# Seven basis units before the softmax in place of two value tiles, one value tile in each of the first four attention steps, and a new front

## The reference

```
h = relu(layernorm(x));  x = x + layer(h)
L0  q, k, v = h Wq + bq, h Wk + bk, h Wv + bv        8 heads of 64
    attn = softmax(q k^T / 8, masked by the edges);  o = attn v Wo + bo
    h1 = layernorm(h + o);  layernorm(h1 + relu(h1 W1 + b1) W2 + b2)
L1  GIN: prelu(h lin^T); twice: (x + sum over edges) -> two linears, batch norm, relu
L2  GCN: normalised sum over edges, W, leaky relu
L3  two RGCN layers, 2 relations: w[r] = sum_b att[r, b] basis[b]   (30 bases of 512 x 512)
    messages gate(x_j) * x_j w[r], summed over edges, + x root + bias
```

## Time and profile before

| | |
|---|---|
| median of 3 runs | 458.7 us (457.14 to 459.46) |
| the profiled execution | 456.62 us, span 454.8 us |
| instructions | 6200 |
| PE busy | 438.6 us, 96% |
| DVE busy | 346.3 us, 76% |
| ACT busy | 243.7 us, 54% |
| granted clock of TensorE | full in all 40 slices |
| HBM read | 93.5 MB |

### The profile page before, as it was taken

How to read it: one execution, slowest core, us unless ns; L and a number is a source line. 1 busy time by engine, 2 the same in 40 slices (tenths; PEclk the granted TensorE clock), 3 DMA queues, 4 the chain that set the end, 5 groups by cost and what they waited for, 6 DMA issues and landing times.

```text
span 454.8 us, 6200 instructions
## 1 busy us (share of the span) xinstructions
PE 438.6 (96%) x2226; PEld 274.3 (60%) x2226; DVE 346.3 (76%) x736; ACT 243.7 (54%) x428; POOL 42.9 (9%) x59
## 2 busy tenths in 40 slices
PE   8999999899997899999999999999998999999997
PEld 3334554443432346768776866677465788888885
DVE  5999996899999968688779657675759695866212
ACT  5999994676897617543345436544534623511210
POOL 3240000024223011000010000010000000000000
PEclk9999999999999999999999999999999999999999
DMA  7997347426699859978099766777973550000002
GB/s 254 415 398 176 110 174 308 179 93 219 235 380 353 295 206 332 409 272 345 11 372 404 295 246 251 275 252 267 375 199 115 225 186 1 1 0 2 0 3 92
DMA packets 18090, 99.22 MB, mean 218 GB/s; under 512 B 2959, under 2 KB 3599, under 8 KB 7567
## 3 DMA queue, kind: packets, MB, share of 16 engines
q1 hardware_dynamic: 13191, 72.72, 43.4%
q0 software_dynamic: 4000, 25.18, 15.1%
q10 hardware_dynamic: 864, 0.86, 0.6%
HBM read 93.50 MB, written 5.25 MB: 217 GB/s over the span
## 4 chain that ended last, share of the span: by engine, by line
PE 70%; DVE 12%; DMA 8%; issue 8%; ACT 1%; POOL 0%; DVEq 0%; POOLq 0%
PE bank L1371 15%; PE sbank L1703 10%; PE bank L1716 6%; PE sbank L1357 6%; PE sbank L1427 6%; PE bank L1608 5%; DMA bring<-in_basis 4%; PE bank L1688 4%; PE sbank L1567 3%; PE bank L1450 3%; DMA wring<-in_weights 3%; PE bank L1357 3%; PE bank L1513 2%; PE sbank L1337 2%; PE sbank L1490 2%
## 5 line engine op out<-in xcount | busy, mean ns | idle before, releaser
L839 DVE TENSOR_SCALAR cnt<-iota_row,edge_f 128x512 bf16<-128x512 f16 x132 | 41.4, 350 | 0.4 <-PE sbank L1427 0.4
L1357 PE MATMUL sbank<-bring,attw 120*32 120x512 f32 x336 | 41.0, 599 | 0.1
L1427 PE MATMUL sbank<-cnt,adjT 128*128 128x512 bf16 x132 | 30.6, 380 | 0.3
L466 ACT ACTIVATE stat<-stat,eps 128x1 f32<-128x1 f32 x32 | 9.4, 294 | 39.3 <-DVE stat L858 39.3
L576 ACT ACTIVATE adjT<-distance,edge_w,edge_f 128x128 bf16<-128x128 bf16 x61 | 29.2, 479 | 1.4 <-PE sbank L1427 1.4
L1281 DVE SCALAR_TENSOR_TENSOR y_lo<-sbank,gate,y_hi 128x512 fp32r<-128x512 f32 x16 | 11.8, 750 | 22.6 <-ACT y_hi L765 22.5
L497 ACT ACTIVATE s<-bank,colsb 128x512 f32<-128x512 f32 x24 | 16.4, 687 | 21.8 <-PE bank L1371 21.8
L1427 PEld LDWEIGHTS sbank<-cnt,adjT 128*128 128x128 bf16 x132 | 12.3, 98 | 21.7 <-DVE cnt L839 6.4
L529 ACT ACTIVATE distance<-iota_row,edge_f 128x128 bf16<-128x128 f16 x61 | 24.3, 400 | 1.8 <-DVE edge_f L905 0.4
L1371 PE MATMUL bank<-hT_hi,w_hi 128*128 128x512 f32 x64 | 25.3, 395 | 0.0
L1371 PE MATMUL bank<-hT_hi,w_lo 128*128 128x512 f32 x64 | 24.9, 390 | 0.0
(11 more groups left out here) (250 smaller groups left out, 1092.5 us busy)
## 6 DMA issues: line engine op xcount, KB each, us to landing
bring<-in_basis SPq DMA_DIRECT2D x59, 1024.0 KB, 9.8
wring<-in_weights POOLq DMA_DIRECT2D x8, 1024.0 KB, 10.0
landing<-in_weights POOLq DMA_DIRECT2D x4, 1024.0 KB, 5.1
w_scratch<-stage SPq DMA_DIRECT2D x16, 256.0 KB
hT<-in_weights POOLq DMA_DIRECT2D x4, 1024.0 KB, 9.1
qkw<-w_scratch POOLq DMA_DIRECT2D x2, 2048.0 KB, 7.9
rring<-in_rows POOLq DMA_DIRECT2D x12, 256.0 KB, 8.5
wring<-in_basis SPq DMA_DIRECT2D x2, 1024.0 KB, 12.9
```

The costliest lines, as they stand in the source:

```text
L839: dve.tensor_scalar(hot_s[:, n % HOT, :], iota[:, :], src_f[:, n:n + 1], None, ALU.is_equal).then_inc(sem("hot_ready"), 1)
L1357: mm = pe.matmul(unit_bank(b)[32 * j:32 * j + 32, :], attw[0:KB, u // UNITS, g, :], unit_place(u)[0:KB, j, :], start=(g == 0), stop=(g == ...
L1427: pe.matmul(bank[7][:, :], hot_d[:, n % HOT, :], hot_s[:, n % HOT, :], start=(n == 0), stop=(n == ECH - 1)).then_inc(sem("hot_used"), 1)
```

## The change

1. **Front.** All four x tiles go on SP's queue. ACT's queue carries dst, then src (semaphore `edges_loaded`), then the edge type, which now counts on `cols_loaded`. DVE does four of the eight edge steps ahead of the norm statistics, after waiting for dst and src.
2. **Units for value tiles.** `FIRST_UNITS = (4, 3)`: four units stand between `products(0, 0)` and `exclude(0, 0)`, and three after the count check, where value tiles 0 and 1 stood. The value tiles go to steps 0 to 3, one each, all in bank 3; `STEP_UNITS` becomes (2, 0, 0, 0, 3, 3, 3, 0). The sum of units up to the end of the attention is the same (26). Batch 3 has bank 1. The first unit of batch 5 waits for all value tiles.
3. **DVE, ACT and POOL of it.** `take_v(it-1)` stands in steps 1 to 4, after the sum over heads and ahead of `find_max`. ACT copies batches 2 and 3 in step 0, behind the exponentials of step 1. `attend(0)` waits for batch 3's copy. The load of row g2 on POOL moves behind step 4.
4. **GCN.** `units(6)` stands for `units(5)` and `keep_clock(4)`; a later `units(2)` is `units(1)`. The GCN product goes tile by tile (`BY_TILE`). The low part of root1 is made on POOL (`low_parts`), not on DVE.

```diff
-STEP_UNITS = (1, 2, 3, 3, 3, 3, 3, 0)
+FIRST_UNITS = (4, 3)
+STEP_UNITS = (2, 0, 0, 0, 3, 3, 3, 0)
 def unit_bank(b):
+            if b == EARLY_UNITS // BATCH + 1:
+                return bank[1]
 # SP
-                for c in (0, 2):
+                for c in range(C):
                     sp.dma_start(xr[:, c, :], x[:, c, :]).then_inc(sem(f"x{c}_loaded"), 16)
 # POOL
+                def low_parts(name, ks=range(C)):
+                    hi, lo = weight_parts(name)
+                    i = IN_PARTS.index(name)
+                    for k in ks:
+                        pool.wait_ge(sem("weight_hi"), i * C + k + 1)
+                        if i and k == 0:
+                            pool.wait_ge(sem("weight_parts"), i * C)
+                        pool.tensor_tensor(lo[:, k, :], weight(name)[:, k, :], hi[:, k, :].bitcast(F32),
+                                           ALU.subtract).then_inc(sem("weight_parts"), 1)
...
-                scale_heads(0)
-                scale_heads(1)
-                load_row("g2", "v")
-                for it in range(2, 2 * C - 1):
+                for it in range(2 * C - 1):
                     scale_heads(it)
+                    if it == C:
+                        load_row("g2", "v")
...
                 load_weight("root1")
+                low_parts("root1")
                 load_w(0)
 # ACT
-                for c in (1, 3):
-                    act.dma_start(xr[:, c, :], x[:, c, :]).then_inc(sem(f"x{c}_loaded"), 16)
-                for i, e in enumerate((src, dst, etype)):
+                for i, e in ((1, dst), (0, src)):
                     act.dma_start(edge_i[:, i, :], e).then_inc(sem("edges_loaded"), 16)
+                act.dma_start(edge_i[:, 2, :], etype).then_inc(sem("cols_loaded"), 16)
...
-                    stage_units(STEP_UNITS[it])
+                    stage_units(STEP_UNITS[it] + (0 if it else sum(FIRST_UNITS)))
 # DVE, ahead of the norm statistics
+                dve.wait_ge(sem("edges_loaded"), 32)
+                ... (dst & 127, dst >> 7, src_f, then dst_lo; taken out of their place below)
...
                 centre(0)
-                take_v(0)
-                take_v(1)
                 for it in range(2 * C):
...
+                    if 1 <= it <= C:
+                        take_v(it - 1)
...
-                    if it < 2:
-                        take_v(2 + it)
...
                     T_lo("agg2", c)
-                split_weight("root1")
 # PE
-                        if g == 0 and b == EARLY_UNITS // BATCH:
-                            pe.wait_ge(sem("v"), 1)
-                        elif g == 0 and b == EARLY_UNITS // BATCH + 1:
+                        if g == 0 and b == EARLY_UNITS // BATCH + 3:
                             pe.wait_ge(sem("v"), C)
...
                 products(0, 0)
-                qkv_tile(2 * C)
+                units(FIRST_UNITS[0])
                 pe.wait_ge(sem("no_edge"), 1)
                 exclude(0, 0, "scores_psum")
...
-                qkv_tile(2 * C + 1)
+                units(FIRST_UNITS[1])
                 pe.wait_ge(sem("flag"), 1)
...
-                    if it:
+                    if it == 0:
+                        units(1)
+                    else:
+                        if it == 1:
+                            pe.wait_ge(sem("stage_ready"), EARLY_UNITS // BATCH + 2)
                         attend(it - 1)
...
-                    if it < 2:
-                        qkv_tile(2 * C + 2 + it)
-                    units(STEP_UNITS[it])
+                    if it < C:
+                        qkv_tile(2 * C + it)
+                    units(STEP_UNITS[it] - (it == 0))
...
-                units(5)
-                keep_clock(4, bank[4])
+                units(6)
...
-                parts_stage("gcn", hT_parts, "agg2", "gcn_psum", t_major=False)
+                parts_stage("gcn", hT_parts, "agg2", "gcn_psum", order=BY_TILE, t_major=False)
...
-                units(2)
+                units(1)
                 turn_rel(0, "h_rel0", 1)
```

More of the change, by code:

```diff
@@ L90 @@
 RING_UNITS = [n for n in range(2 * UNITS) if not in_extra(n)]
-STEP_UNITS = (1, 2, 3, 3, 3, 3, 3, 0)
-ATTENTION_BATCHES = (EARLY_UNITS + sum(STEP_UNITS)) // BATCH + 1
+FIRST_UNITS = (4, 3)
+STEP_UNITS = (2, 0, 0, 0, 3, 3, 3, 0)
+ATTENTION_BATCHES = (EARLY_UNITS + sum(FIRST_UNITS) + sum(STEP_UNITS)) // BATCH + 1
 AGG0_BATCHES = 11
@@ L293, in wait_unit @@
             pe.wait_ge(sem(f"basis{r % BATCH}_loaded"), 16 * (r // BATCH + 1))
-        def v_bank(c):
-            return 3 if c else 2
         def place_of(h):
@@ L583, in _ @@
                         if t == 0:
-                            act.wait_ge(sem("cols_loaded"), 32)
+                            act.wait_ge(sem("cols_loaded"), 48)
                         qk_take(t)
@@ L874, in take_v @@
                     dve.wait_ge(sem("v_psum"), c + 1)
-                    dve.tensor_tensor(vr[:, c, :], bank[v_bank(c)][:, :], row("bv"), ALU.add).then_inc(sem("v"), 1)
+                    dve.tensor_tensor(vr[:, c, :], bank[3][:, :], row("bv"), ALU.add).then_inc(sem("v"), 1)
+                dve.wait_ge(sem("edges_loaded"), 32)
+                dve.tensor_scalar(dst_part[:, 0, :], edge_i[:, 1, :], P - 1, None, ALU.bitwise_and).then_inc(
+                    sem("edge_step"), 1)
+                dve.tensor_scalar(dst_part[:, 1, :], edge_i[:, 1, :], P.bit_length() - 1, None,
+                                  ALU.logical_shift_right).then_inc(sem("edge_step"), 1)
+                dve.tensor_copy(src_f, edge_i[:, 0, :]).then_inc(sem("edge_step"), 1)
+                dve.wait_ge(sem("edge_step"), 3)
+                dve.tensor_copy(dst_lo, dst_part[:, 0, :]).then_inc(sem("edge_step"), 1)
                 for c in range(C):
@@ L888, in _ @@
                                     bank[c][:, :].rearrange("p (f n) -> p f n", f=C)).then_inc(sem("hT0"), 1)
[L890 to L895, removed]
+                dve.wait_ge(sem("cols_loaded"), 48)
                 dve.tensor_scalar(rel1, edge_i[:, 2, :], 0.0, None, ALU.not_equal).then_inc(sem("edge_step"), 1)
-                dve.wait_ge(sem("edge_step"), 4)
-                dve.tensor_copy(dst_lo, dst_part[:, 0, :]).then_inc(sem("edge_step"), 1)
+                dve.wait_ge(sem("edge_step"), 5)
                 dve.scalar_tensor_tensor(field, rel1, float(C), dst_part[:, 1, :], ALU.mult, ALU.add).then_inc(
@@ L918, in _ @@
                         dve.tensor_scalar(never[:, :], ident[:, :], NEVER, None, ALU.mult).then_inc(sem("never_bq8"), 1)
-                        dve.wait_ge(sem("cols_loaded"), 32)
+                        dve.wait_ge(sem("cols_loaded"), 48)
                         dve.tensor_scalar(bq8[:, :], col("bq", 0, C), HD ** -0.5, None, ALU.mult).then_inc(
@@ L1438, in qkv_tile @@
                     elif which:
-                        pe.wait_ge(*((sem("v"), c) if c >= 2 else (sem("k"), C)))
-                    at = v_bank(c) if which == 2 else c
+                        pe.wait_ge(*((sem("v"), c) if c else (sem("k"), C)))
+                    at = 3 if which == 2 else c
                     if which == 1:
@@ L1476, in _ @@
                 NH = N // 2
-                pe.wait_ge(sem("cols_loaded"), 32)
+                pe.wait_ge(sem("cols_loaded"), 48)
                 def products(it, pair):
```

## The result

The changed kernel takes 470.12 us (median of 4 runs, 468.55 to 470.46), the one before 459.08 in the runs beside it: a ratio of 1.0234, 95% interval 1.0209 to 1.026, some 11 us slower. The forecast was 459.6, its range ended at 462.0.

What follows compares the result with a forecast made beforehand. PE was taken as busy 438.6 of 454.8 us, with DVE setting the attention's pace. Front -0.4, attention +1.5 and GCN -0.2 summed to +0.9 us: 459.6 us for the median, eight in ten between 455.7 and 462.0.

Steps and rivals of the forecast that it cites:

- Front: From start to first one-hot: reordered edge steps and loads give -0.4 us (bounds -0.6 and +0.3), carried over whole.
- GCN: GCN part: unit 60's wait is nearly offset by DVE's earlier first tile; -0.2 us, bounds -2.6 and +1.
- Three waits: PE gaps claimed at unit 11's load, ACT's copy before unit 16, and unit 60's load: 1.9, 2.4, 3.1 us.
- The step that failed: End of attention: DVE's last step opens 4.7 us late, its last product ends 1.5 late; attention sum +1.5 us.
- The lateness itself: DVE's attention steps: the last, step 7, was to open at 153.9 against 149.2, 4.7 us late.
- about 88.1: Before step 1's scores: time unit 14's load was to land, queued behind units 11 to 13.
- rival (b): New PE gaps drop the clock, one or two warm-ups; +2.8 to +4.7 us, 461.5 to 463.4; chance 0.12.
- It decides from the gap at unit 60: GCN part: the 3.1 us PE gap at unit 60 was to decide whether the clock drops.
- A refill alone takes 4.7, and 3.8 us of waits go: Attention steps 4 to 6: ring full by 105, four of nine units already loaded, so old load waits of 3.8 us vanish.
- It costs nothing if they land before x: DVE's head: the new wait for dst and src was allowed 0 to 0.5 us, being small loads first on their queue.
- The gain of -2.6: GCN part without unit 60's wait: product ends at 347.5 instead of 350.1; the lower bound of that term.

Runs made afterwards that it cites:

- e14: Kernel before with the attention edits (item 2, 3), but FIRST_UNITS (3, 3) and STEP_UNITS (2, 1, 1, 1, 3, 2, 2, 0): ratio 1.0152 to the kernel before.
- e18: e14 with ACT's copy take_ao(1) moved ahead of root(1, 1): ratio 1.0045 to the kernel before.
- e16: The changed kernel with ACT's copy take_ao(1) moved ahead of root(1, 1): ratio 1.0204 to the kernel before.
- e10: Kernel before with the attention edits alone, plus matmuls on zeros ahead of units 11, 12, 14, 16 and project(2): ratio 1.0147 to the kernel before.
- e2: Kernel before with the attention edits alone (units for value tiles, with their DVE, ACT and POOL edits): ratio 1.0208.
- e4: The changed kernel with matmuls on zeros in five PE waits (front, units 11, 14, 16, 60): 465.76 us, ratio 1.0165 to the kernel before.
- e1: Kernel before with the front edits alone (queues of x, edges and edge type; four edge steps ahead of the statistics): ratio 1.0033.
- e5: Kernel before with only the front's new DMA queues, DVE's order as it was: ratio 1.0029.
- e11: Kernel before with all GCN edits, plus 14 matmuls on zeros ahead of unit 60: ratio 1.0002.
- e6: Kernel before with only the GCN tile order and POOL's low parts, units and zeros as before: ratio 0.9964.
- e17: Kernel before with ACT's copy take_ao(1) moved ahead of root(1, 1): ratio 0.9986.
- e9: Kernel before with the last unit of step 6 (unit 25) moved behind attend(7): ratio 1.0019.
- e8: Kernel before with the attention edits, but FIRST_UNITS (3, 3) and STEP_UNITS (2, 1, 0, 0, 3, 3, 3, 0): ratio 1.0098.
- e12: Kernel before with only root1's low part on POOL in place of DVE, GCN product in its old order: ratio 0.9988.

## Why the prediction was wrong

**Three waits were read right.** Predicted 1.9 us for unit 11, 2.4 for the copy ahead of unit 16, 3.1 for unit 60; measured 2.02, 2.25, 3.37.

**The step that failed:** "Behind it 3.7, 1.9 and 3.7 us (project, attend, project) lie before `attend(7)`, and DVE's last product ends 6.9 after the opening, at 160.8; it starts there, where it started at 159.3. Sum for the attention: +1.5 us". There 4.7 us of lateness on DVE became 1.5 by slack on PE. The reckoning ended one instruction too soon: behind `attend(7)` comes `project(2)`, which waits for ACT behind DVE's statistics, 13.1 us after the opening in nine kernels. This chain had no slack, and lateness passes on whole. That is the 3.2 us, shown by the table and by e14 and e18. In the changed kernel itself PE had no slack either: late unit loads kept `project(0)` until 160.50, some 2.4 us behind DVE's release (in e14 that comes 2.55 us ahead of the last opening), so PE's own work would have let `project(2)` start only 1.2 us earlier, about what e16 gained. In e14, without those load waits, the chain alone holds PE by 3.1.

**The lateness itself was mis-sized.** From `products(0, 0)` on, the changed kernel's last opening is 11.45 - 2.67 = 8.8 us late (products at 77.70 for 75.03), not 4.7. The openings between, at 95.39, 103.70, 116.02 and so on, tell where. The second is 3.0 late, predicted 1.2: unit 14 is there at 92.88 - 2.67 = 90.2, not at "about 88.1", and step 1's scores stand behind it. That isn't the clock: in e10 this opening is 2.8 late too (100.83 for 98.00). Step 1 takes 12.3 us for the 10.9 predicted, and this is the clock, since e10 has 10.98. Steps 2 to 6 take 44.7 for 43.8. Together 4.7 + 1.8 + 1.4 + 0.9 = 8.8. (e2, whose clock was full in step 1, has 11.05 there.)

**The clock** was rival (b), at a chance of 0.12 and with one or two warm-ups. The profiled execution had four, and gaps of 2.0 to 2.3 us, about what I had computed for the attention (1.9 and 2.4), were enough. One costs less than I had from the earlier trace rows: 3.2 to 4.4 us for all of them (e4), about 1 each and not 1.9. Which gaps cost also changes between executions: that of e16 has the same front and no drop there. The step wrong here is "It decides from the gap at unit 60".

**The late loads.** "A refill alone takes 4.7, and 3.8 us of waits go": no wait stands between 130 and 149, but waits of 1.00 and 1.33 us come at 150.05 and 159.50. The ring is full from 109 on and its loads start only when units are used again. e14 shows the cure, and that it is worth nothing while DVE's chain holds `project(2)`.

**Front.** Predicted -0.4, measured +1.4 (e1). "It costs nothing if they land before x": DVE got src at 6.41 us (5.77 in e1), while x's statistics start at 4.36 in e5, with the same queues. Everything on DVE stood behind that wait, PE waited 2.46 us for the first turn, and the first one-hot came 2.0 us later (14.06 for 12.04), not half a us earlier; in e1 it came 1.4 later. The quarter size of the load said nothing of when it lands. That this wait is all of the +1.4 isn't shown, since e5, without it, measured nearly the same time.

**GCN.** Predicted -0.2, measured +0.6 (0.9995 to 1.0052), and 1.0002 with the clock up (e11): without the drop of the clock the sum was right. The gain of -2.6 that was expected without unit 60's wait was 1.6 (e6). POOL took 5.95 us for its four parts (predicted 4.8), and DVE's add took 1.66 beside it in place of 0.69. By the Trainium skill's GPSIMD Engine Reference (section 1) they share the interface for two SBUF inputs; the run agrees, by 1.0 us on one instruction. It doesn't undo the gain (e6).

**The sum again**, by what the runs gave: front +1.4; attention +6.8 by DVE's last opening without the clock (e10: 156.08 for 149.23), passed on whole, and +2.8 by the clock; GCN +0.6. That is 11.6 for the measured 11. The two profiled executions differ by more, 13.6 us. Some 0.9 of it lies between 225 and 250, where PE takes 17.4 us in place of 16.5 from a group of four units to the last turn of the stage (236.46 to 253.86, before 225.04 to 241.58). That isn't the change: e17, which moves one line of ACT, takes 17.7, and 17 of the 20 traces take 17.2 or more. The profiled execution of the kernel before, 2.1 us under its median, is one of the three quick ones.

## What to carry to other kernels

Before crediting slack on one engine, follow each late event to the end of every chain that starts in it, also past the instruction that was late before: two chains that end within 0.2 us of each other look like one in a profile, and moving either alone gained nothing here. Price a new gap on TensorE at its length plus a possible clock drop, even at 2 us, and keep idle filler where a real unit of work would have to wait for its load. A wait placed at the head of an engine's order delays all that stands behind it until its load lands, however small the load is. Before reading a difference of 1 us between two profiles, look for it in a third kernel that doesn't have the change.

## What the runs showed of the hardware

- In the changed kernel gaps of 2.02, 2.25, 2.46 and 3.37 us were followed by the lower clock, one of 2.23 wasn't. In e9 one of 2.10 was, in e8 one of 2.59, in e14 one of 2.67; but in e1 one of 2.67 and in e16 one of 2.87, both behind the zeros of the front, were not (the next eight matmuls took 1.27 us, in the changed kernel 1.94). In the profiled execution of e12 the clock fell after waits of 1.47, 0.92 and 1.31 us for loads, with units between them (`project(0)` took 5.94 us for 3.70). Length alone doesn't decide.
- A load of 66 KB (src) issued at 1.19 us was there 5.2 us later in the changed kernel and 4.6 in e1; a tile of x four times as large, issued at 0.74 on the other queue, was there after 3.6 (e5, DVE at 4.36).
- DVE's add of two SBUF tiles, 0.69 us alone, took 1.66 beside POOL's subtraction; POOL's four took 5.95, 1.49 each.
